# q and k of two units in one pass, and one transposition moved: a graph-attention kernel on one Trainium2 core

## The reference, cut to what matters

```
q, k, v = heads(x @ Wq + bq), heads(x @ Wk + bk), heads(x @ Wv + bv)
scores  = where(adj > 0, q @ k.T / sqrt(HD) + beta * adj, -9e15)
h       = layernorm(x + softmax(scores) @ v)
for l in (0, 1):                        # inner layers, on h
    a    = softmax(h @ h.T / sqrt(384)) * adj;  a = a / sum(a)
    ctx  = upper(a) @ (h @ Wl.T + bl) + diag(a) * (h @ Ws.T + bs) + lower(a) @ (h @ Wr.T + br)
    h'   = relu(layernorm(ctx) * g + b)
out     = layernorm(h + h')             # h: the input of the inner layers
```

## Time and profile before

| | |
|---|---|
| median of 3 runs | 1282.96 us |
| the profiled execution: its time, its span | 1282.98 us, 1281.2 us |
| PE busy in the span | 99% |
| DVE, ACT, POOL busy | 77%, 49%, 29% |
| granted clock, mean | 0.996 |

### The profile page before, as it was taken

The page is one execution under the profiler, slowest core; times in us unless marked ns, Lnnn a source line. Parts: engine busy times, 40 slices in busy tenths (PEclk is TensorE's granted clock), DMA queues, the critical chain, the costliest instruction groups (busy, mean ns, idle before and its releaser), DMA issues.

```text
span 1281.2 us, 34717 instructions
## 1 busy us (share of the span) xinstructions
PE 1263.4 (99%) x13844; PEld 1166.7 (91%) x13844; DVE 990.4 (77%) x2691; ACT 632.6 (49%) x1338; POOL 370.6 (29%) x401
## 2 busy tenths in 40 slices
PE   9999999999999999999999999999999999999986
PEld 8999999999999999999999999999999999999975
DVE  6777778777878777787778787777877777877877
ACT  6544554544554445545445545455454455454543
POOL 3322323232323222323223232223232232323211
PEclk9999999999999999999999999999999999999989
DMA  8211110111110111110111101111101111011000
GB/s 275 85 39 57 58 57 25 35 57 57 57 57 4 55 57 57 57 28 31 57 58 58 57 15 44 57 57 57 43 16 57 57 58 58 20 39 45 26 14 26
DMA packets 53072, 66.34 MB, mean 52 GB/s; under 512 B 17840, under 2 KB 39856, under 8 KB 52784
## 3 DMA queue, kind: packets, MB, share of 16 engines
q1 hardware_dynamic: 52768, 63.93, 16.5%
q10 hardware_dynamic: 144, 0.20, 0.0%
HBM read 38.54 MB, written 12.58 MB: 40 GB/s over the span
## 4 chain that ended last, share of the span: by engine, by line
PE 97%; DVE 1%; issue 1%; ACT 1%; POOL 0%; POOLq 0%; DVEq 0%; ACTq 0%
PE bank L420 25%; PE bank L422 23%; PE bank L421 23%; PE bank L623 7%; PE bank L569 4%; PE bank L532 4%; PE bank L517 3%; PE bank L498 3%; PE bank L545 2%; PE bank L555 2%; PE bank L603 1%; PE bank L631 0%; DVE probs L1222 0%; POOL probs L1727 0%; PE bank L745 0%
## 5 line engine op out<-in xcount | busy, mean ns | idle before, releaser
L420 PE MATMUL bank<-w_hi,hT_hi 128*128 128x384 f32 x1158 | 405.4, 350 | 0.2 <-ACT hT_hi L1048 0.2
L422 PE MATMUL bank<-w_hi,hT_lo 128*128 128x384 f32 x1158 | 390.3, 337 | 0.0
L421 PE MATMUL bank<-w_lo,hT_hi 128*128 128x384 f32 x1158 | 390.1, 337 | 0.0
L420 PEld LDWEIGHTS bank<-w_hi,hT_hi 128*128 128x128 f32 x1158 | 218.3, 189 | 6.6 <-issue 2.0
L421 PEld LDWEIGHTS bank<-w_lo,hT_hi 128*128 128x128 f32 x1158 | 218.9, 189 | 0.0
L422 PEld LDWEIGHTS bank<-w_hi,hT_lo 128*128 128x128 f32 x1158 | 218.3, 189 | 0.0
L1293 DVE TENSOR_TENSOR hlr<-bank,rows 128x384 f32<-128x384 f32 x256 | 142.3, 557 | 70.9 <-PE bank L422 68.0
L1740 POOL TENSOR_TENSOR ln_rstd<-ln_var,minus_half 128x2 f32<-128x2 f32 x125 | 96.2, 769 | 322.1 <-DVE ln_var L1386 113.8
L1727 POOL TENSOR_TENSOR probs<-probs,row_max 128x768 f32<-128x768 f32 x64 | 94.6, 1478 | 265.7 <-DVE row_max L1228 265.7
L1310 DVE TENSOR_TENSOR late<-bank,rows 128x384 f32<-128x384 f32 x128 | 71.3, 558 | 118.0 <-PE bank L422 117.9
L420 PE MATMUL bank<-xT_hi,w_hi 128*128 128x256 f32 x558 | 158.7, 284 | 0.0
(11 more groups left out here) (131 smaller groups left out, 2370.9 us busy)
## 6 DMA issues: line engine op xcount, KB each, us to landing
v_halves<-v_stage SPq DMA_DIRECT2D x128, 99.0 KB, 2.3
x_in<-in_x SPq DMA_DIRECT2D x32, 384.0 KB, 4.0
xT_in<-in_xT SPq DMA_DIRECT2D x31, 384.0 KB, 3.4
out<-late SPq DMA_DIRECT2D x31, 384.0 KB, 2.4
late<-in_w SPq DMA_DIRECT2D x7, 576.0 KB, 6.5
adj_in<-in_adj SPq DMA_DIRECT2D x32, 96.0 KB, 3.8
adjT_in<-in_adjT SPq DMA_DIRECT2D x64, 48.0 KB, 3.2
rows<-in_vectors SPq DMA_DIRECT2D x1, 1536.0 KB, 8.7
```

Source lines behind the costliest of these rows:

```text
L420: nc.tensor.matmul(o, l_hi, r_hi, start=first and n == 0, stop=False)
L421: nc.tensor.matmul(o, l_hi, r_lo, start=False, stop=False)
L422: done = nc.tensor.matmul(o, l_lo, r_hi, start=False, stop=final and n == last)
```

## The change

Two edits.

q and k are made for two units at a time. Unit 0 is made alone in `begin`, as before. Then set p holds units 2p-1 and 2p; the last set, 16, holds unit 31 alone. A set has six groups (q and k for each m); one group is nine matmuls whose moving operand is the x^T of both units, 512 columns in two pieces of 256, and fills one bank. Set 1 is made whole in `second`; every later step makes three groups of a set, at the places where the three calls stood: a step with even early unit u makes groups 0 to 2 of the set of u+1, a step with odd u groups 3 to 5 of the set of u. So q and k of a unit are ready one to two steps earlier than needed. They live in `q_first`, `q_second`, `k_first`, `k_second` with slots for this. `xT_hi` and `xT_lo` have three slots, and x^T is loaded and split two units further ahead (LOAD = 5, SPLIT = 4 in place of 3 and 2). In `second` three units are split (1 and 2 first, 3 last), and v of unit 1 moves from behind q and k to ahead of them. The scalar engine makes the same number of take instructions for a whole set, two per group.

The second edit: in a full step `transpose_e` of layer 1 moves on PE from ahead of the first self product to behind it, directly ahead of `transpose_h`; on DVE `mask_aT` moves between the two `self_bias` instructions. `transpose_h` waits for the last take of the step in the new counting. The last line of the diff makes the reserve for descriptors of software-made transfers smaller, which leaves room for the larger tiles.

```diff
@@ helpers
+SPLIT, LOAD = 4, 5
+X_SLOTS = 3
+GROUPS = 2 * KC
+def qk_set(unit):
+    return (unit + 1) // 2
+def set_units(p):
+    first = max(2 * p - 1, 0)
+    return [u for u in (first, first + 1) if u < UNITS and qk_set(u) == p]
+def x_slot(unit):
+    return (unit - 1) % X_SLOTS
+def step_groups(unit):
+    return [(qk_set(unit + 1), j) if unit % 2 == 0 else (qk_set(unit), KC + j) for j in range(KC)]
@@ tiles
-        kT = sb("kT", [P, KC, TOK])
+        k_first = sb("k_first", [P, 1, 3, TOK])
+        k_second = sb("k_second", [P, 2, 2, TOK])
-        xT_hi = sb("xT_hi", [P, KC, TOK], F32R)
-        xT_lo = sb("xT_lo", [P, KC, TOK], F32R)
-        qT = sb("qT", [P, KC, TOK])
+        xT_hi = sb("xT_hi", [P, KC, X_SLOTS, TOK], F32R)
+        xT_lo = sb("xT_lo", [P, KC, X_SLOTS, TOK], F32R)
+        q_first = sb("q_first", [P, 2, 3, TOK])
+        q_second = sb("q_second", [P, 1, 2, TOK])
@@ SP: begin and second
-                load_xT(st, EARLY + 1)
+                load_xT(1)
+                load_xT(2)
...
-                load_xT(st, EARLY + 1)
+                load_xT(3)
                 raw_weight(8)
+                load_xT(4)
@@ PE: the products of a set
+            def project_qk(st, p, j):
+                units, m = set_units(p), j // 2
+                pe.wait_ge(xhi_ready, units[-1] + 1)
+                pe.wait_ge(xlo_ready, units[-1] + 1)
+                if p == 1:
+                    if j == 0:
+                        need(pe, s_masked, st.count(MID, 4, 4))
+                    if j >= 2:
+                        pe.wait_ge(qk_ready, qk_taken(p, j - 2))
+                elif j % KC == KC - 1:
+                    pe.wait_ge(qk_ready, qk_taken(p, j - 1))
+                o = group_bank(p, j)[:, 0:len(units) * TOK].rearrange("p (u n) -> p u n", u=len(units))
+                done = product(o, [(weight((W_Q, W_K)[j % 2], kc, m * P, (m + 1) * P), x_of_set(p, kc)) for kc in range(KC)])
+                done.then_inc(qk_psum, 1)
@@ PE: second
+                project_v(st, EARLY)
+                project_qk(st, 1, 0)
+                project_qk(st, 1, 1)
                 transpose_probs(st)
-                project_qk(st, 1)
+                project_qk(st, 1, 2)
                 attend(st)
-                project_qk(st, 2)
-                project_v(st, EARLY)
+                project_qk(st, 1, 3)
+                project_qk(st, 1, 4)
+                project_qk(st, 1, 5)
                 transpose_h(st)
                 scores(st, EARLY)
@@ PE: a full step
                     project_v(st, EARLY)
-                    project_qk(st, 0)
-                    project_qk(st, 1)
+                    project_qk(st, *groups[0])
+                    project_qk(st, *groups[1])
...
-                    project_qk(st, 2)
+                    project_qk(st, *groups[2])
...
                     project_sides(st, 1)
+                    project_self(st, 1, 0)
                     transpose_e(st, 1)
-                    project_self(st, 1, 0)
                 if mid:
                     transpose_h(st)
@@ ACT: takes
+            def take_qk(st, p, j):
+                m = j // 2
+                act.wait_ge(qk_psum, qk_made(p, j))
                 need(act, s_psum, st.count(MID, 1, 1))
+                for unit in set_units(p):
+                    bias, scale = (bk_col, 1.0) if j % 2 else (bq_col, SCALE_ATT)
+                    nc.scalar.activation(group_out(unit, j), group_half(unit, group_bank(p, j)), ACT.Identity,
+                                         bias=bias[:, m:m + 1], scale=scale).then_inc(qk_ready, 1)
@@ DVE: a full step
                     sides_bias(st, 1, 1, RIGHT)
+                    self_bias_tile(st, 1, 0)
                     mask_aT(st, 1)
-                    self_bias(st, 1)
+                    self_bias_tile(st, 1, 1)
@@ the program
-    nc = bacc.Bacc("TRN2", target_bir_lowering=False, num_devices=1)
+    nc = bacc.Bacc("TRN2", target_bir_lowering=False, num_devices=1, dynamic_dma_scratch_size=4096)
```

More of the change, by code:

```diff
@@ L1096, in step @@
                     return
+                if early:
+                    groups = step_groups(st.unit(EARLY))
                 if late and st.unit(LATE) == 0:
@@ L1778, in step @@
                     return
-                if early and not st.unit(EARLY) == 0:
-                    split_x(st)
+                if st.unit(EARLY) == 0:
+                    return
+                if st.unit(MID) == 0:
+                    second(st)
+                    return
+                if st.has(SPLIT):
+                    split_x(st.unit(SPLIT))
                 if mid:
```

182 lines of the change are left out of this document (104 added, 78 removed).

## The result

The changed kernel takes 1286.65 us (8 runs, 1285.95 to 1287.33) against 1282.47 us (8 runs, 1281.38 to 1283.35): a ratio of 1.0033, interval 1.0023 to 1.0044. The profiled execution has a span of 1285.5 us (before 1281.2) at a mean granted clock of 0.996.

What follows compares the result with a forecast made beforehand. PE, busy 99% of the span, was taken to bound the kernel. Full steps -3.2, edit of e -0.2, fill +5.2, steps 28 and 29 -2.4 make -0.6 us against 1282.98: 1282.4 us, range 1275.0 to 1286.5.

Steps and rivals of the forecast that it cites:

- Full steps: Steps 0 to 27: q and k cost 6.18 us a step, 0.12 less than before; -3.2 us over 28 steps.
- 512 columns cost 0.229 us: Price of one q and k matmul on PE, taken between readings of 0.2269 and 0.2315 us; bounds 0.2133 and 0.2354.
- Rival (C): Full steps: reads of 512 columns are the limit, 0.2328 to 0.2340 us each, so nothing gained, 1286.5 us; chance 0.16.
- All three ways of reading the rows of 256 and 384: Price of 512 columns: addition stays, 0.2269 us; goes with the columns, 0.2315; straight line through both widths, 0.2295.
- Edit of e: Full steps, layer 1: joining two runs of transpositions saves 0.2 us over 28 steps, and the mix does not wait.
- The fill: Before step 0: 6.15 us of added q and k, 1.2 of waits hidden, 0.3 of new wait; +5.2 us.
- Steps 28 and 29: Last steps with an early unit: 3.15 us of work leaves each, uncovered waits take about 1.9; -2.4 us for both.
- The end of the range: Upper end of the forecast for the whole kernel's time: 1286.5 us, leaving out the far end of Rival (C).
- the fill's own upper bound of +8: The fill's worst case: x^T of unit 2 is 3 us late beyond the cover; the lower bound was +4.

Runs made afterwards that it cites:

- e1: Separate kernel computing nothing of the reference: runs of 24 matmuls at several widths, fp32r and bf16, operands starting alike; 512 columns fell into 226.7 ns in fp32r, 215.8 in bf16.
- e7: Separate kernel computing nothing of the reference: matmuls with operands at chosen bytes of one large tile; 512 columns took 226.6 to 237.1 ns.
- e6: Separate kernel computing nothing of the reference: fp32r matmuls with weights and x^T at the changed kernel's places in SBUF; 512 columns took 233.3 to 233.4 ns.
- e8: The changed kernel with x^T's two tiles allocated ahead of `v_halves`, so that they start like the weights within 256 bytes: 1283.87 us, ratio 1.0009.
- e9: The kernel before with x^T's two tiles allocated ahead of `v_halves`, the same edit as e8: 1288.16 us, ratio 1.0043.
- e2: The kernel before with the second edit alone (transposition of e behind the first self product, mask between the self biases): 1282.73 us, ratio 0.9997.
- e4: The changed kernel with ACT's split of x^T of unit 3 in the fill moved directly behind the split of weight 5, POOL's pass following: 1287.62 us, ratio 1.0040.
- e13: e8 with x^T of unit 3 loaded ahead of `move_v`, the row vectors and weights 6 and 7, and with e4's early split: 1284.16 us, ratio 1.0012.

## Why the prediction was wrong, by its steps

- **Full steps (-3.2 us): this step failed, with the term "512 columns cost 0.229 us".** It is 0.2336, so the steps gained nothing from the width. Of the 4.9 us between forecast and profile 3.1 are this term in steps 1 to 27. Rival (C) had the size right (0.2328 to 0.2340, 1286.5 us) with 0.16. Its reason holds only in part: with the operands alike the addition is 13 ns at 256, 384 and 512 columns (e1), so the reads of 512 columns are no limit as such; but at 192 bytes it does grow with the columns, 11, 17 and 20 ns (e7: 117.9, 176.6, 233.4). All three ways of reading the rows of 256 and 384 assumed that the price is a function of the width. It was in fact the price at two different distances of operands' starts, 192 bytes for q and k and 64 for the side and self products of the earlier trace rows (e6, e7), and 256 columns gain from 192 bytes where 512 lose. That the place decides in the kernel too, e8 and e9 show. Why it does, no run shows.
- **Edit of e (-0.2).** Right, and as small as forecast (e2). The mix of layer 1 has no wait in full steps; joining the runs of transpositions costs nothing.
- **The fill (+5.2, then -0.1 for step 0): it was +6.8.** The first Gram of step 0 came at 39.66 for the 39.0 forecast, 5.9 later than before; the transpositions of the probabilities had no idle entry, and the scores waited 0.27 for `k_second` where 0.3 was forecast. Of the 0.7 us that it is late, 0.35 are from the very start, where the stretch at half clock in unit 0 was longer (256 columns stood 0.213 us apart until 7.75, before until 6.80; from kernel to kernel its end differs by 2 us), and 54 x 4.6 ns = 0.25 are the price of 512 columns again. The larger miss, 1.0 us, is in step 0, which took 41.13 us where it took 40.19 and 0.1 less was forecast. Its first side products take 0.8 more, with a stall of 0.63 that did not exist before, and the transpositions of z and of the probabilities 0.3 more (they took 0.5 too long before as well); the mix waits for 0.39, which is less than the 0.55 before. POOL's split of unit 3 now falls on DVE's `u_bias`, and where it does not (e4, e13) the mix and the transpositions have no wait, while the stall is longer: its cause stays open. I had priced the splits' move at nothing for the full steps, where that is true, and not looked at what they meet in step 0. Undoing the meeting made step 0 0.9 us shorter in the profile of e4, but no version kept that in its time: e4 and e13 lost as much or more elsewhere.
- **Steps 28 and 29 (-2.4): right**, 1.20 us each, and with the three waits that were forecast: 0.46 ahead of the probabilities, 0.21 for `pT`, 0.68 for `hT_lo` (0.7, 0.2 and 0.8 forecast).
- **The end of the range.** The sum of known costs, fill plus last steps, was +2.8 us whatever the width did; a width that brings nothing was thus near +2.6 by itself, and the range, which ended at +3.5, should have reached past it by the fill's own upper bound of +8. The 0.2% taken as the least that can be told was too much as well: the interval of the measured ratio is 0.1% to either side.
- **What it would take.** With the operands alike the change comes to within 0.0 to 0.18% of the kernel before (e8). No version here beats the kernel before; its 256 columns are by chance near their best distance.

## What to carry over

A price per matmul read from a trace belongs to a width and to the places of the operands: before extrapolating to a wider one, ask how the moving operand and the weights start against one another, and put a short run of the new width, at the places it will have, beside the old. Work moved into the fill of a full engine is paid at once, and comes back at the end only as far as no chain is uncovered: here 2.4 of 6.3 us. A moved pass of POOL should be laid against DVE's short operations at its new place.

## What the hardware showed that was not expected

- The distance of fp32r matmuls depends on the starts of moving operand and weights modulo 256 bytes: 226.6 to 233.4 ns at 512 columns in steps of 64 bytes, up to 237.1 at 4 bytes; 173.3 to 178.5 at 384; 116.4 to 122.2 at 256 (e7, moving operand shifted). Absolute place (0 to 156 KB) and order of the operands cost nothing.
- A stream has several such distances and falls into one: 256 columns at one and the same place run at 117.8 ns behind 384 columns and at 113.4 behind transpositions, and stay there as long as the run lasts, for 27 matmuls in e6.
- With the operands alike fp32r adds 13 ns to the bare columns at 256, 384 and 512, bf16 2.5. Below 256 columns it hardly gets cheaper: 192 and 128 columns took 111.5 ns each (e1).
